# Row statistics and weights taken a stage ahead, fewer filler products, and the last attention segment divided on chip

## The reference

```python
def norm(x): return (x - mean(x)) / sqrt(var(x) + 1e-5)   # over the 128 channels, no gain or bias
x += bond_attention(norm(x))   # L0: 16 heads, a window of 64 keys, logits from displacements
x += masked_ffn(norm(x))       # L0: of each 64 hidden units the argmax of a low-rank mask is kept
x += mamba(norm(x))            # L1: selective scan, forward and reversed
x += gated_experts(norm(x))    # L1: softmax over 128 gates, argmax picks 1 of 8 experts, times its prob.
x += dual_attention(norm(x))   # L2: sigmoid(lam)*dense + (1-sigmoid(lam))*sparse top-20% attention, then an ff
x += ternary_ffn(norm(x))      # L2: silu(xW1*s1)*(xW2*s2), two gelu layers, a projection
x += plain_attention(norm(x))  # L3: softmax(q k^T) v, 16 heads of 8, full 2048 x 2048, then w_o
x += int8_ffn(norm(x))         # L3: silu(x Wg) * (x Wu) @ Wd, weights dequantised from int32
```

## Time and profile before

| | us |
|---|---|
| median of 3 runs | 2810.73 (2809.03 to 2813.31) |
| profiled execution | 2809.22 |
| its span in the trace | 2807.0 |
| PE busy | 2330.5 (83%) |
| DVE busy | 2191.4 (78%) |
| ACT busy | 1923.2 (69%) |
| POOL busy | 1077.9 (38%) |

### The profile page before, as it was taken

The page is one execution under the profiler, slowest core; times in us unless marked ns, Lnnn a source line. Parts: engine busy times, 40 slices in busy tenths (PEclk is TensorE's granted clock), DMA queues, the critical chain, the costliest instruction groups (busy, mean ns, idle before and its releaser), DMA issues. The chain is left out here.

```text
span 2807.0 us, 46788 instructions
## 1 busy us (share of the span) xinstructions
PE 2330.5 (83%) x19221; PEld 973.1 (35%) x19221; DVE 2191.4 (78%) x3012; ACT 1923.2 (69%) x2056; POOL 1077.9 (38%) x423
## 2 busy tenths in 40 slices
PE   5677777788856777786799988999879989999996
PEld 1122222255322323244233342333544533333334
DVE  5788888868799999976789848997640368899984
ACT  4999999942654343334599948997432379999982
POOL 5999999912059999922000500014100000000000
PEclk8899999879978899998899999999989989999998
DMA  2011111120134544401402110001010030210000
GB/s 79 1 46 46 46 54 53 56 76 1 34 115 166 178 166 172 142 9 59 71 14 29 28 28 2 13 15 48 9 43 0 22 85 17 45 36 17 16 10 27
DMA packets 67165, 145.54 MB, mean 52 GB/s; under 512 B 13683, under 2 KB 30431, under 8 KB 66240
## 3 DMA queue, kind: packets, MB, share of 16 engines
q1 hardware_dynamic: 66944, 142.47, 17.8%
HBM read 117.99 MB, written 24.25 MB: 51 GB/s over the span
## 5 line engine op out<-in xcount | busy, mean ns | idle before, releaser
L828 POOL TENSOR_TENSOR l0a_diff_pool<-l0a_A,l0a_a_of_t 128x2048 f32<-128x2048 f32 x128 | 531.7, 4202 | 32.2 <-ACT l0a_a_of_t L843 29.6
L2147 ACT ACTIVATE l2x_pT<-ps 128x1024 f32<-128x1024 f32 x512 | 470.3, 1163 | 11.2 <-PE ps L2105 11.1
L2299 ACT ACTIVATE l3he_pT<-ps 128x1024 f32<-128x1024 f32 x480 | 445.1, 1064 | 16.8 <-PE ps L2233 16.8
L774 DVE SCALAR_TENSOR_TENSOR l0a_diff_dve<-l0a_A,l0a_pos,ps 128x512 f32<-128x512 f32 x512 | 344.7, 739 | 31.0 <-PE ps L619 31.0
L1469 PE MATMUL ps<-l1s_hc,all_ident 128*128 128x512 f32 x512 | 272.4, 685 | 95.1 <-POOL l1s_hc L1420 90.4
L1411 POOL TENSOR_TENSOR l1s_dBx<-l1a_dtx,l1a_Bs 128x1024 f32<-128x1024 f32 x128 | 298.2, 2371 | 78.8 <-POOLq L1134 78.8
L2105 PE MATMUL ps<-l2m_Qs,l2m_Ks 75*32 75x512 bf16 x4096 | 273.1, 385 | 13.3 <-DMA l2m_Qs<-l2m_mparts 8.9
L2233 PE MATMUL ps<-l3h_Qs,l3h_Ks 75*32 75x512 bf16 x4096 | 273.8, 383 | 7.0 <-DVE ps L2304 6.9
L2120 PE MATMUL ps<-l2x_pT,l2m_Va 128*9 128x512 f32 x2048 | 268.6, 597 | 7.8 <-ACT l2x_pT L2147 2.8
L860 ACT ACTIVATE l0a_diff_pool<-l0a_diff_pool 128x2048 f32<-128x2048 f32 x128 | 237.3, 1901 | 26.7 <-POOL l0a_diff_pool L828 26.6
L2244 PE MATMUL ps<-l3he_pT,l3h_Va 128*9 128x512 f32 x1920 | 250.4, 595 | 1.2
(11 more groups left out here) (497 smaller groups left out, 3696.0 us busy)
## 6 DMA issues: line engine op xcount, KB each, us to landing
l1a_Bs<-l1a_bc SPq DMA_DIRECT2D x64, 512.0 KB, 3.6
l1s_Cs<-l1a_bc SPq DMA_DIRECT2D x64, 512.0 KB, 4.6
l0a_band_rows<-l0a_band SPq DMA_DIRECT2D x32, 512.0 KB, 7.0
l0a_band<-l0a_exps SPq DMA_DIRECT2D x14, 512.0 KB
l2m_Ks<-l2m_parts SPq DMA_DIRECT2D x36, 128.0 KB
l2m_Qs<-l2m_parts SPq DMA_DIRECT2D x72, 64.0 KB
l3h_Qs<-l3h_parts SPq DMA_DIRECT2D x72, 64.0 KB
l0a_band<-l0a_zero SPq DMA_DIRECT2D x8, 512.0 KB, 7.4
```

The costliest lines, as they stand in the source:

```text
L774: ins = dve.scalar_tensor_tensor(out[:, c, :], src[:, c, :], pos[:, d:d + 1], bank(1), ALU.add, ALU.subtract)
L828: pool.tensor_tensor(out, window(s), atb[:, p % 2, :].unsqueeze(1).broadcast_to([P, 4, CH]), ALU.subtract).then_inc(diff_pool, 1)
L2147: act.activation(pT[:, turn % NPT, :], g.ps[:, slot * QC:(slot + 1) * QC], ACT.Exp).then_inc(expd, 1)
L2299: act.activation(pT[:, (4 * m + j) % NPT, :], g.ps[:, slot(turn)], ACT.Exp).then_inc(expd, 1)
```

## The change

- Statistics for ln1, ln2, ln3, ln4, ln6 and ln7 are taken by DVE in the stage ahead, after its writes to x; the openings then begin with epsilon. masked_ffn, gated_experts and ternary_ffn do it block by block (with a lag of 4, 4 and 1 blocks), bond_attention and mamba after their quarter adds.
- keep_clock has 6 products instead of 20 where the statistics are known.
- early_root: one square root on one column, at the end of ACT's stream in the stage ahead (at its beginning in masked_ffn).
- mamba's 18 loads are issued by SP in masked_ffn's main block, dual_attention's 21 in gated_experts' after its own four. The factor sigmoid(lam) is made in gated_experts as 1/(1+exp(-lam)): POOL scales three small tensors ahead of its iota, ACT takes the exponential after quarter 0's, DVE adds one and takes the reciprocal after quarter 0, POOL weighs the bias row at block 8. The separate small block of dual_attention is gone.
- stack_first stands before the wait for V and its store.
- head_attention's last segment doesn't go through DRAM: PE transposes oT, DVE divides, PE puts it upright into partitions 96 to 127, ACT and DVE copy it to OT; projection, adds and statistics follow in the same block.

```diff
@@ layer norm, both forms
-                if transposed and load is not None and tag != "ln0":
-                    keep_clock(pe, g, 7 * CH, 20)
+                if transposed:
+                    keep_clock(pe, g, 7 * CH, 6 if known else 20)
@@ bond_attention, DVE
+                    if w >= 2 and off == 30 and hf == 1:
+                        dve.wait_ge(x_done, q)
+                        row_stats.of(dve, g.X, range(4 * q - 4, 4 * q))
+                        row_stats.gather(dve, range(4 * q - 4, 4 * q))
...
+                dve.wait_ge(x_done, NCH)
+                row_stats.of(dve, g.X, range(TB - 4, TB - 2))
+                row_stats.gather(dve, range(TB - 4, TB - 2))
                 late_add(1)
+                dve.wait_ge(x_done, NCH + 1)
+                row_stats.of(dve, g.X, range(TB - 2, TB))
+                row_stats.gather(dve, range(TB - 2, TB))
@@ masked_ffn
+            @block.sync
+            def _(sp):
+                ahead.load(sp)
+                sp.wait_ge(ahead.loads, 16 * ahead.n)
...
+                def statistics(b):
+                    dve.wait_ge(xad, b + 1)
+                    row_stats.of(dve, g.X, range(b, b + 1))
+                    if b % 4 == 3:
+                        row_stats.gather(dve, range(b - 3, b + 1))
                 for b in range(TB + 1):
                     if b < TB:
                         mask(b)
                     if b:
                         pick(b - 1)
+                    if b >= 4:
+                        statistics(b - 4)
+                for b in range(TB - 3, TB):
+                    statistics(b)
@@ mamba, after each quarter's add to x
+                        dve.wait_ge(xad, (q + 2) % 4 + 1)
+                        row_stats.of(dve, g.X, range(4 * q, 4 * q + 4))
+                        row_stats.gather(dve, range(4 * q, 4 * q + 4))
@@ gated_experts, SP, POOL, ACT, DVE
                 ln.sync(sp)
+                ahead.load(sp)
+                sp.wait_ge(ahead.loads, 16 * ahead.n)
...
+                ahead.scale(pool)
                 pool.iota(pri[:, :], [[-1, C]], base=C, channel_multiplier=0, allow_small_or_imprecise_dtypes=True).then_inc(const, 1)
                 for b in range(TB):
+                    if b == TB // 2:
+                        ahead.weigh_bias(pool)
...
                     exps(q)
+                    if q == 0:
+                        ahead.exponential(act)
...
                     dve.tensor_tensor(y[:, b % 4, :], z[:, k, 0, :], z[:, k, 1, :], ALU.add).then_inc(yd, 1)
+                    if b >= 4:
+                        statistics(b - 4)
...
+                    if q == 0:
+                        ahead.sigmoid(dve)
+                for b in range(TB - 4, TB):
+                    statistics(b)
@@ DualWeights
+    def scale(self, pool):
+        pool.wait_ge(self.loads, 16 * self.n)
+        pool.tensor_scalar(self.lam[:, 1:2], self.lam[:, 0:1], -1.0, None, ALU.mult).then_inc(self.scaled, 1)
+        pool.tensor_scalar(self.bqk[:, 0:1], self.bqk[:, 0:1], self.QS, None, ALU.mult).then_inc(self.scaled, 1)
+        pool.tensor_scalar(self.bp[:, 0:1], self.bp[:, 0:1], self.R ** -0.5, None, ALU.mult).then_inc(self.scaled, 1)
@@ dual_attention, half 0, SP
+                                hd.stack_first(sp)
                                 sp.wait_ge(vcp, 1)
                                 sp.dma_start(vdram, V[:, :, :]).then_inc(vst, 16)
-                                hd.stack_first(sp)
                                 sp.wait_ge(vst, 16)
@@ ternary_ffn, DVE, the last loop
                     if t >= 1:
-                        dve.wait_ge(xad, t)
+                        statistics(t - 1)
+                statistics(TB - 1)
@@ head_attention, PE after the last segment
+                for c in range(2):
+                    pe.wait_ge(accr[c], NSEG)
+                    for j in range(4):
+                        at = (4 * c + j) * P
+                        mm = pe.transpose(g.ps[:, 2 * CH + at:2 * CH + at + P], oT[:, (NSEG - 1) % 2, at:at + P], g.ident[:, :])
+                    mm.then_inc(turned, 1)
...
+                for b in range(TB // 4):
+                    project(b, b * P)
+                for c in range(2):
+                    pe.wait_ge(divided, c + 1)
+                    for j in range(4):
+                        at = (4 + c) * CH + j * P
+                        mm = pe.matmul(g.ps[LAST_ROWS, at:at + P], oN[:, c, j, :], g.ident[:, :], start=True, stop=True)
+                    mm.then_inc(upright, 1)
...
+                for b in range(TB // 2, TB):
+                    if b % 4 == 0:
+                        pe.wait_ge(last_ready[b // 4 - 2], 1)
+                    project(b, ACC + (b - TB // 2) * P)
@@ DVE after the last segment
-                finish(NSEG - 1)
+                for c in range(2):
+                    dve.wait_ge(turned, c + 1)
+                    rows = g.ps[:, (2 + c) * CH:(3 + c) * CH].rearrange("p (b j e) -> p b j e", b=4, j=4)
+                    dve.reciprocal(rd[:, c, :, :], rows[:, :, :, HS:HS + 1].rearrange("p b j e -> p b (j e)")).then_inc(inverted, 1)
...
+                add(0, 0)
+                dve.wait_ge(upright, 2)
+                dve.tensor_copy(OT[LAST_ROWS, QC + CH:T], g.ps[LAST_ROWS, 5 * CH:6 * CH]).then_inc(last_ready[1], 1)
+                add(1, CH)
+                statistics(0)
+                add(2, ACC)
+                statistics(1)
+                add(3, ACC + CH)
+                statistics(2)
+                statistics(3)
```

More of the change, by code:

```diff
@@ L91, in _, with early_root @@
             dve.memset(g.eps[:, :], 1.0e-5).then_inc(ready, 1)
+def early_root(act, g):
+    act.activation(g.early_root[:, :], g.eps[:, :], ACT.Sqrt)
 def keep_clock(pe, g, at, count):
@@ L903, in _, with masked_ffn @@
                     sp.wait_ge(loaded[b], 16 * NPH)
-def masked_ffn(nc, g, I):
+def masked_ffn(nc, g, I, ahead):
     D1, D2, DL = 8, 64, 64
@@ L1012, in _ @@
             def _(act):
+                early_root(act, g)
                 for q in range(NCH):
@@ L1070, in mamba, with ffn_and_mamba @@
+def ffn_and_mamba(nc, g, I):
+    with ExitStack() as ctx:
+        weights = MambaWeights(nc, ctx, I)
+        masked_ffn(nc, g, I, weights)
+        clear_semaphores(nc)
+        mamba(nc, g, weights)
+def mamba(nc, g, weights):
+    R = R1
+    win, wout, cw, cb, wx, wdt = weights.win, weights.wout, weights.cw, weights.cb, weights.wx, weights.wdt
+    bdt, Al, Dp = weights.bdt, weights.A, weights.D
     with ExitStack() as ctx:
         r = Room(nc, ctx, "l1a")
-        win = r.sb("win", [C, 2 * DI])
@@ L2273, in _ @@
                 hd.stack_second(sp)
-                for seg in range(NSEG):
+                for seg in range(NSEG - 1):
                     hg, qc = divmod(seg, NQ)
@@ L2299, in _ @@
                         act.activation(pT[:, (4 * m + j) % NPT, :], g.ps[:, slot(turn)], ACT.Exp).then_inc(expd, 1)
+                early_root(act, g)
+                act.wait_ge(upright, 1)
+                act.copy(OT[LAST_ROWS, QC:QC + CH], g.ps[LAST_ROWS, 4 * CH:5 * CH]).then_inc(last_ready[0], 1)
             @block.vector
@@ L2483, in dual_attention, with gated_and_dual @@
+def gated_and_dual(nc, g, I):
+    with ExitStack() as ctx:
+        weights = DualWeights(nc, ctx, I)
+        gated_experts(nc, g, I, weights)
+        clear_semaphores(nc)
+        dual_attention(nc, g, I, weights)
+def dual_attention(nc, g, I, weights):
     R, DFF = 64, 512
@@ L3211, in load @@
             return 2
[L3212 removed]
+        layernorm_transpose(nc, g, "ln6", load, known=True)
         OT = r.sb("OT", [C, T])
         hid = C ** -0.5
[L3215 to L3229 removed]
+        head_attention(nc, g, "l3h", w, None, hid * 8 ** -0.5, hid, hid * (S / (S - 1.0) ** 0.5) * S ** -0.5 * hid, wo, OT)
 def store_output(nc, g, out):
@@ L3242, in _ @@
                 sp.wait_ge(stored, 16)
-LAYERS = (bond_attention, masked_ffn, mamba, gated_experts, dual_attention, ternary_ffn, plain_attention, int8_ffn)
+LAYERS = (bond_attention, ffn_and_mamba, gated_and_dual, ternary_ffn, plain_attention, int8_ffn)
 def clear_semaphores(nc):
```

234 lines of the change are left out of this document (132 added, 102 removed).

## The result

The changed kernel takes **2777.73 us** (median of 4 runs, 2776.39 to 2780.25) against 2810.72: a ratio of 0.9886 (95% interval 0.9873 to 0.9898), 1.1% faster. The span is 2774.65 against 2807.05, 32.4 less. Forecast were 2783 and −26.8.

The account below looks back on a forecast made before the run. No engine was over 83% busy; DVE chains and waits held the openings, and DVE bound the masked_ffn and gated_experts loops. Terms summed to −26.8 from 2809.2, giving 2782.4 (2783.9 by the median), stated as 2783, range 2768 to 2798.

Parts of the forecast that it names:

- H: stack_first in dual_attention: transfers issued earlier end before PE's first reader needs them, store of V queues behind; −4.8 us (to 0).
- K: plain_attention's end: last segment kept on chip, without DRAM round trip and the 6.55 us reciprocal; −11.0 us (−14 to −8).
- F: dual_attention's opening: statistics, wait for loads and small block gone, transposes at slow clock; −8.2 us (−7 if these cost more).
- A: masked_ffn's opening: −4.4 for statistics gone, +0.8 behind bond_attention's last add, +0.4 for slow transposes; −3.2 us (−4.4 to 0).
- G: PE's clock in dual_attention's head_prepare: less slow clock once the wait of 4.9 is gone; −1.5 us (−2.4 to 0).
- B: masked_ffn's DVE-bound loop takes in 12 statistics and three aggregations; +3.9 us (0 if gaps take them, +6 with semaphore waits).
- E: gated_experts' loop and end take in statistics, aggregations and sigmoid's two short operations on DVE; +3.6 us (0 to +6).
- rival 3: The moved statistics are hidden in masked_ffn, gated_experts and mamba's tail: −9 more, 2774; chance 0.12.
- D: mamba's end +2.0 for statistics; gated_experts' iota waits behind 21 loads, its reader at S+15.3, 2.0 later; +4.0 us (−2.4 to +5).
- I: ternary_ffn's opening: 6 fillers for 20 let transposes begin earlier, less 0.8 for slow clock; −3.3 us (−4.1 to 0).
- L: int8_ffn's opening: dequantisation waits for loads, so only −0.3 arrives, and PE starts slow, +1.4; +1.1 us (−0.3 to +5).
- Rival 1: Fewer fillers leave PE slow in the seven openings and first products behind them: +14, 2797; chance 0.18.

Follow-up runs that it names:

- the doubled set: Changed kernel with masked_ffn's statistics taken twice, the second set into tensors that nothing reads: median 2782.24 us (+4.5).
- the control: The changed kernel run once more without an edit: median 2776.87 us, four runs from 2772.32 to 2781.16.
- the one with the DRAM end: Changed kernel with the last attention segment through DRAM again, projections in a block of their own, statistics behind each add: median 2795.32 us (+17.6).

## Why the prediction was right

The time, 2777.7, lies in the range and 5.3 under the forecast; 32.4 instead of 26.8 were gained in the profiles. The mechanisms of H, K and the openings are the ones that the experiments show; F's rests on the timeline. Part of the closeness is luck: the clock's terms were mis-sized in both directions (A and G gained more than forecast, two stretches lost where nothing was), and the start and the stretch before masked_ffn's first mid, together 4.2 of the gain beyond the forecast, come out otherwise in other kernels whose code there is the same.

- *Statistics, B, C, J* were sized right: 0.20 for one, most of it paid in masked_ffn (the doubled set: +3.0 of 4.3, the set that is there: +4.0 for 4.6 in B and C), −4.4 in each opening. In masked_ffn and mamba together the move is worth 0.7.
- *E* was right by sum (+3.0 for +3.6) and wrong by content: without the statistics the stage is 1.6 shorter, so rival 3 was half right there. And with 20 fillers, where the statistics are in the loop too, it is only 0.5 longer than before (59.6 for 59.1 from the iota's reader on). From the ninth block's y to the stage's end, in before, in the changed kernel and with 20 fillers (columns as in the earlier trace rows):

```profile
1259.60:1284.89 25.29, 13.10 (x42) 5.69 (x41) 18.52 (x40) 11.43 (x48) 14.60 (x24) 0.92 0.00 0
```

```profile
1256.62:1284.99 28.37, 16.40 (x45) 6.60 (x43) 22.28 (x64) 13.11 (x49) 14.41 (x24) 0.80 0.00 0
```

```profile
1267.05:1293.48 26.43, 13.11 (x42) 5.69 (x42) 21.48 (x63) 12.92 (x49) 14.62 (x24) 0.91 0.00 0
```

All of the +3.0 lies there, and 2.0 of it goes with PE's clock, 0.80 instead of 0.92 and 0.91. I had put all of it on DVE.
- *D*: the mechanism was right, the wait mis-sized: from the last issue to POOL's release it took 3.25, where the step had 2.1, so the reader was at S+16.6 instead of S+15.3.
- *F* was right: −8.2. *H* was right in size and by its mechanism: −4.6. The batch took 30.4 in before, where the step had 28.5. The assumption that the store of V waits for all stacked transfers was half wrong. The windows ahead of its issue and behind it:

```profile
1335.00:1339.36 4.36, 3.92 (x26) 2.50 (x25) 2.32 (x2) 0.46 (x1) 0.00 (x0) 1.00 0.51 71
1339.36:1344.36 5.00, 2.42 (x10) 0.99 (x12) 4.81 (x6) 2.15 (x3) 0.00 (x0) 0.99 0.77 187
```

The rate rose from 71 to 187 GB/s: of the store's 128 packets of 8192 bytes 64 started within 3.2 us of its issue, among the batch. The other 64 started only from 8.2 to 11.7 us after it, when the batch's last packets ran, and the control shows the same halves. All had landed 25.9 us after the block's begin, where I had some 34. The Trainium skill (DMA: Bandwidth & Descriptors, "Two DMAs through the same engine are not ordered") says that the descriptors of one queue of an engine start in order but are pipelined; that a store starts only when all transfers ahead of it are done doesn't follow from it, and the trace doesn't show it.
- *K*: −11.9 for −11.0. The statistics took the 4.8 of the step. The first add (0.7) stood ahead of the copies of the upright products, and the sum had put it behind them.
- *I* and *L*: I put PE at the slow clock behind few fillers at +0.8 and +1.4. Six fillers and transposes at the slow clock are there (2.90 and 2.98 in masked_ffn), but ACT's normalisation sets the pace, and it cost nothing in L.
- *The term that was mis-sized most is the clock, in A and G.* I let it cost +0.4 in A and gain 1.5 in G. Between masked_ffn's first product and first mid it gained 3.15 (1.12 for 2.07), in head_prepare 3.0. It cost 1.1 and 2.1 in the rest of dual_attention and in plain_attention, where I had nothing. These four make −1.5 of the 5.6. A's tail and transposes (−1.2), I and L (−1.8), K (−0.9), B (−0.6) and E (−0.6) go the same way, D (+1.1) the other. A's part isn't safe: the start took 612.2 to 614.4 in the thirteen profiles with this code, 612.36 in the one compared.

Rival 1 fell: the first products after short openings were fast, and head_prepare's 16 went from 9.54 to 7.10. By the Trainium skill's rule that the slow clock is the default and activity releases it (TensorE: Matmul & The Clock Gate, "What's actually happening") I named fillers as what holds the clock. The trace agrees with the rule (the clock was 0.66 in the six us behind the iota's wait, where before had 1.00), and 20 fillers do make the transposes faster. What the rule doesn't say is the balance: the 4.4 us that they take are more than the 1.0 that they give in an opening and the 2.5 that they gave behind one. Why the first products behind the short openings were fast in most kernels and slow in the one with the DRAM end, whose code is the same there, stays open. Rival 2 didn't occur (the clock was 0.97 from masked_ffn's first to its last mid, as before), nor rival 4.

## What to carry to other kernels

Filler work that is there for PE's clock must be shortened together with what it covers: here it was worth 18.6 of the 33 us, and moving the statistics alone would have left the fillers as the new bound. An operation moved to an idle moment of another engine takes its wait with it, and all that stands behind it there; put it behind what others wait for. Move work out of an opening into a stage that its engine doesn't bound; in a stage that it does bound the move pays back what it gains.

## What the runs showed of the hardware

One profile is less certain than the run times are, and for two reasons. One is the granted clock: identical code in gated_experts took 28.4 and 31.6 us (clock 0.92 and 0.77). Such stretches come in few values, not in a spread: before masked_ffn's first mid −3.15 against before in ten kernels (clock 1.00), 0.0 in three (0.77, as in before), and one of these three is identical to the changed kernel up to there. The other is the landing of a DMA that the next one waits for: from plain_attention's first product to its first scores it took 36.3 and 39.4 at nearly the same clock (0.80 and 0.78), as SP waited 2.3 and 6.2 us for one small store. A small edit's worth is then better read from its own stretch than from the span, as long as the clock and the DMA waits in that stretch are given beside it.
